# TensorE adds the experts' results and the residual in the last stage of a graph layer with experts

## The reference

```python
h = feats * rsqrt(deg_out)[:, None]
m = segment_sum(h[src], dst, n) * rsqrt(deg_in)[:, None]
x = (m @ W_gc + b_gc) + (feats @ W_res + b_res)
core = moe_ff(x, ...)        # each node's two best of 64 experts, weighted by their gates
y = x + core
mean = y.mean(axis=0); var = ((y - mean) ** 2).mean(axis=0)
out = (y - mean) * rsqrt(var + 1e-5) * gamma + beta
z = feats + out
result = (z - z.mean(axis=-1)) / sqrt(z.var(axis=-1) + 1e-5)
```

## Time and profile before

| | |
|---|---|
| median of three runs | 3374.38 us (3372.07 to 3375.9) |
| the profiled execution | 3370.39 us, its span 3368.7 us, 1.7 us around it |
| mean granted clock of TensorE | 0.940 |
| busy, share of the span | PE 83%, DVE 59%, ACT 36%, POOL 63% |
| `norms` | from about 3186 us to the end: 182 us |

### The profile page before, as it was taken

The page is one execution under the profiler, slowest core; times in us unless marked ns, Lnnn a source line. Parts: engine busy times, 40 slices in busy tenths (PEclk is TensorE's granted clock), DMA queues, the critical chain, the costliest instruction groups (busy, mean ns, idle before and its releaser), DMA issues. The chain is left out here.

```text
span 3368.7 us, 60861 instructions
## 1 busy us (share of the span) xinstructions
PE 2787.4 (83%) x15086; PEld 2055.8 (61%) x15227; DVE 1991.0 (59%) x6954; ACT 1201.6 (36%) x2876; POOL 2136.8 (63%) x2168
## 2 busy tenths in 40 slices
PE   4756888888888898888988889859999999999750
PEld 4534555555555555555555555539889889988640
DVE  6994555545555555555555556555555555555698
ACT  5982222222222222222222222214444444444339
POOL 5886777777777777777777777735555555555300
PEclk8877999999999999999999999979999999999885
DMA  7457454554545545455454554534444544444377
GB/s 238 150 180 229 134 160 136 158 168 135 158 137 158 168 135 159 138 157 167 135 160 135 158 168 126 162 119 131 157 137 140 165 144 132 145 145 134 136 300 250
DMA packets 305867, 533.96 MB, mean 159 GB/s; under 512 B 47156, under 2 KB 216729, under 8 KB 304046
## 3 DMA queue, kind: packets, MB, share of 16 engines
q0 software_dynamic: 102576, 273.86, 27.7%
q1 hardware_dynamic: 202734, 256.32, 22.8%
q10 hardware_dynamic: 400, 1.84, 0.2%
HBM read 416.19 MB, written 119.91 MB: 159 GB/s over the span
## 5 line engine op out<-in xcount | busy, mean ns | idle before, releaser
L1298 POOL DMA_INDIRECT work<-h_table,src_cols x1543 | 1466.3, 950 | 484.5 <-issue 461.2
L1688 PE MATMUL ps<-work 128*128 128x257 f32 x3322 | 1067.0, 404 | 244.2 <-DMA work<-h_table,src_cols 208.4
L1688 PEld LDWEIGHTS ps<-work 128*128 128x128 f32 x3322 | 574.3, 192 | 614.1 <-issue 472.8
L1830 POOL DMA_INDIRECT picked<-ys,places x228 | 250.0, 1097 | 357.7 <-DVE ys L1900 339.0
L1559 PE MATMUL ps<-none_w,none 128*128 128x512 bf16 x1244 | 476.3, 383 | 0.0
L1955 PEld LDWEIGHTS ps<-xst,work 128*128 128x128 f32 x3648 | 443.5, 192 | 28.0 <-issue 15.9
L1955 PE MATMUL ps<-xst,work 128*128 128x128 f32 x3648 | 447.3, 276 | 10.7 <-issue 10.0
L1962 PE MATMUL ps<-work,hid 128*128 128x256 f32 x1824 | 436.2, 382 | 0.3
L1811 ACT ACTIVATE hid<-ps,b_cols 128x128 f32<-128x128 f32 x912 | 316.7, 367 | 160.7 <-PE ps L1955 114.6
L1962 PEld LDWEIGHTS ps<-work,hid 128*128 128x128 f32 x1824 | 328.9, 190 | 45.7 <-ACT hid L1811 10.1
L1365 DVE TENSOR_TENSOR logits<-ps,gate_bias 128x64 f32<-128x64 f32 x98 | 22.0, 224 | 541.2 <-ACT acc L1253 541.2
(11 more groups left out here) (293 smaller groups left out, 4060.9 us busy)
## 6 DMA issues: line engine op xcount, KB each, us to landing
work<-in_L_gnn_w_dram SPq DMA_DIRECT2D x128, 512.0 KB, 4.6
picked<-work SPq DMA_DIRECT2D x14, 1792.0 KB, 8.1
work<-h_table,src_cols POOLq DMA_INDIRECT x1543, 2.8
pk<-picked SPq DMA_DIRECT2D x13, 1792.0 KB, 9.9
acc<-m_base SPq DMA_DIRECT2D x14, 903.0 KB, 4.9
x_beta<-xr_x SPq DMA_DIRECT2D x98, 128.0 KB
pk<-x_beta SPq DMA_DIRECT2D x14, 896.0 KB, 7.2
xr_x<-in_x_dram SPq DMA_DIRECT2D x97, 128.0 KB, 2.5
```

The lines of the kernel that those rows point to most:

```text
L1298: pool.indirect_dma_start(out=got[:, c % RING, 0:D], out_offset=None, in_=h_table[:, :], in_offset=bass.IndirectOffsetOnAxis(ap=src_cols[: ...
L1688: mm = nc.tensor.matmul(ps_flat[:, bank(t, k, w[0])], hot[:, (2 * t + (k >= HALF)) % HOTS, k % HALF if k >= HALF else k, :], got[:, c % RI ...
L1830: pool.indirect_dma_start(out=picked[:, :], out_offset=bass.IndirectOffsetOnAxis(ap=places[:, u:u + 1], axis=0), in_=ys[:, u, :], in_offse ...
```

## The change

In `aggregate` the addition of beta to feats becomes a `scalar_tensor_tensor` with an accumulator, so that each row's sum lands in `xb_sum`, kept in SBUF.

In the first pass TensorE takes the experts' results in pairs of tiles: four matmuls with the identity `ident` as weights put the sum of both experts' rows of two tiles into one bank of PSUM (of seven that take turns; the variance moves to the eighth). VectorE adds a pair from PSUM to `acc3` in one instruction of 512 columns, 49 in all; the two additions of seven tiles go. TensorE issues the pairs of group g+1 ahead of the folding of group g's squares. The buffers of `pk` are given back when the pairs are made (`paired`).

In the second pass `times_scale` becomes seven instructions, each of which also gives the row's sum; the mean comes from this sum and `xb_sum`. TensorE puts z = (x + beta) + scaled y into PSUM with two identity matmuls a tile, in two sets of four banks that alternate from group to group, and waits for `normed` of the group two before. ScalarE and VectorE read z from PSUM. ScalarE takes four tiles' deviations, VectorE three by `bn_stats`, with four small instructions to join the halves of each. In VectorE's order `minus_mean(g)` comes ahead of `spreads(g - 1)`, and `deviations(g)` ahead of `shifts(g - 1)`. ScalarE's order stays.

The diff, cut to its core (new semaphores, tiles and changed argument lists are left out):

```diff
@@ -1358,7 +1359,8 @@
...
                 dve.wait_ge(beta_in, 16)
-            nc.vector.tensor_tensor(xt[:, t % 2, :], xt[:, t % 2, :], beta_b[:, :], ALU.add).then_inc(beta_added, 1)
+            nc.vector.scalar_tensor_tensor(xt[:, t % 2, :], xt[:, t % 2, :], 1.0, beta_b[:, :], ALU.mult, ALU.add,
+                                           accum_out=xb_sum[:, t:t + 1]).then_inc(beta_added, 1)
...
@@ -1980,12 +1982,13 @@
...
 B = 4
-ON_ACT = 5
+ON_ACT = 4
 LAST_ON_ACT = 4
...
 UPFRONT = CENTRED + 2
-assert NT % GT == 0 and NG > B
+ZB = (GT + 1) // 2
+assert NT % GT == 0 and NG > B and NT % 2 == 0 and 2 * D <= BANK and 2 * ZB <= 8
 pk = t2("pk", [P, B, GT, TOP_K * D], F32)
...
@@ -2031,11 +2037,20 @@
...
-def adds(g):
-    return len(FIRST_PARTS) + g + (len(LAST_PARTS) - 1) * (g == NG - 1)
+def pairs_to(t):
+    return (t + 1) // 2
...
     return acc3[:, g * GT + u, 0:D]
+
+def pair_sum(i, b=2):
+    return ps[:, i % 7, 0:b * D]
+
+def z(g, u):
+    return ps[:, g % 2 * ZB + u // 2, u % 2 * D:(u % 2 + 1) * D]
+
+def z_ready(g, u):
+    return ZB * g + u // 2 + 1
...
@@ -2053,7 +2068,7 @@
...
             if g >= B:
-                sp.wait_ge(second_added, adds(g - B))
+                sp.wait_ge(paired, pairs_to(GT * (g - B + 1)))
             sp.dma_start(pk[:, g % B, :, :], rows_of(rows, g)).then_inc(pk_in[g % B], 16)
...
@@ -2076,11 +2091,11 @@
...
         for q in range(B):
-            sp.wait_ge(second_added, adds(NG - B + q))
+            sp.wait_ge(paired, pairs_to(GT * (NG - B + q + 1)))
             load_x(q)
...
             if g + B < NG:
-                sp.wait_ge(z_set, g + 1)
+                sp.wait_ge(z_done, ZB * (g + 1))
                 load_x(g + B)
...
@@ -2093,68 +2108,64 @@
...
         nc.vector.tensor_copy(last_ones[:, :], valid[:, NT - 1:NT].broadcast_to([P, P])).then_inc(last_ones_set, 1)
+        nc.vector.tensor_scalar(xb_sum[:, :], xb_sum[:, :], -1.0 / D, None, ALU.mult).then_inc(row_sums_set, 1)
+
         def centre(g):
...
-        def add(g, a, b, n):
-            nc.vector.tensor_tensor(group(g, a, b), group(g, a, b), pk[:, g % B, a:b, 0:D], ALU.add).then_inc(first_added, 1)
-            dve.wait_ge(first_added, n)
-            nc.vector.tensor_tensor(group(g, a, b), group(g, a, b), pk[:, g % B, a:b, D:2 * D], ALU.add).then_inc(second_added, 1)
+        def add(i):
+            dve.wait_ge(paired, i + 1)
+            rows = acc3[:, 2 * i:2 * i + 2, 0:D]
+            nc.vector.tensor_tensor(rows, rows, pair_sum(i).rearrange("p (u d) -> p u d", d=D), ALU.add).then_inc(added, 1)
...
             centre(g)
-        done = 0
-        for g in range(NG):
-            if g >= CENTRED:
-                dve.wait_ge(centred, g - CENTRED + 1)
-            if g > 0:
-                dve.wait_ge(pk_in[g % B], 16 * (g // B + (g % B > 0)))
-            for n, (a, b) in enumerate(FIRST_PARTS if g == 0 else parts(g)):
-                if g == 0:
-                    dve.wait_ge(first_in[n], 16)
-                done += 1
-                add(g, a, b, done)
-            if g + UPFRONT < NG:
-                centre(g + UPFRONT)
+        for i in range(NT // 2):
+            g, last = 2 * i // GT, (2 * i + 1) // GT
+            if last >= CENTRED:
+                dve.wait_ge(centred, last - CENTRED + 1)
+            add(i)
+            if (2 * i + 1) % GT >= GT - 2 and last + UPFRONT < NG:
+                centre(last + UPFRONT)
         dve.wait_ge(sq_used, NG - 1 + len(LAST_PARTS))
-        nc.vector.tensor_scalar(scale[:, :], ps[:, 1, 0:D], 1.0 / N, BN_EPS, ALU.mult, ALU.add).then_inc(var_set, 1)
+        nc.vector.tensor_scalar(scale[:, :], ps[:, 7, 0:D], 1.0 / N, BN_EPS, ALU.mult, ALU.add).then_inc(var_set, 1)
         dve.wait_ge(var_rooted, 1)
...
         dve.wait_ge(scale_set, 1)
-        dve.wait_ge(second_added, adds(NG - 1))
+        dve.wait_ge(added, NT // 2)
+        dve.wait_ge(row_sums_set, 1)
         def times_scale(g):
-            nc.vector.tensor_tensor(group(g), group(g), scale[:, :].unsqueeze(1).broadcast_to([P, GT, D]),
-                                    ALU.mult).then_inc(scaled, 1)
-
-        def residual(g):
-            dve.wait_ge(scaled, g + 1)
-            dve.wait_ge(xb_in[held(g)], 16 * (g // B + 1))
             for u in range(GT):
-                last = nc.vector.scalar_tensor_tensor(tile(g, u), tile(g, u), 1.0, pk[:, held(g), u, D:2 * D], ALU.mult, ALU.add,
-                                                      accum_out=z_sum[:, g % 2, u:u + 1])
-            last.then_inc(z_set, 1)
+                nc.vector.scalar_tensor_tensor(tile(g, u), tile(g, u), 1.0, scale[:, :], ALU.mult, ALU.mult,
+                                               accum_out=z_sum[:, g % 2, u:u + 1]).then_inc(scaled, 1)
         def minus_mean(g):
-            dve.wait_ge(z_set, g + 1)
-            nc.vector.tensor_scalar(z_mean[:, g % 2, :], z_sum[:, g % 2, :], -1.0 / D, None, ALU.mult).then_inc(z_mean_set, 1)
+            dve.wait_ge(scaled, GT * (g + 1))
+            nc.vector.scalar_tensor_tensor(z_mean[:, g % 2, :], z_sum[:, g % 2, :], -1.0 / D, xb_sum[:, g * GT:(g + 1) * GT],
+                                           ALU.mult, ALU.add).then_inc(z_mean_set, 1)
         def deviations(g):
-            dve.wait_ge(z_mean_set, g + 1)
-            if g >= B:
-                dve.wait_ge(o_out[held(g)], 16 * (g // B))
             for u in range(ON_ACT, GT):
-                last = nc.vector.scalar_tensor_tensor(pk[:, held(g), u, 0:D], tile(g, u), z_mean[:, g % 2, u:u + 1], tile(g, u), ALU.add, ALU.mult,
-                                                      accum_out=dev[:, g % 2, u:u + 1])
-            last.then_inc(dev_by_dve, 1)
+                dve.wait_ge(z_done, z_ready(g, u))
+                last = nc.vector.bn_stats(stats[:, u - ON_ACT, :], z(g, u))
+            last.then_inc(stats_set, 1)
+            dve.wait_ge(stats_set, 4 * g + 1)
+            own = dev[:, g % 2, ON_ACT:GT]
+            nc.vector.tensor_tensor(halves_gap[:, 0, :], stats[:, :, 1], stats[:, :, 4], ALU.subtract).then_inc(stats_set, 1)
+            nc.vector.tensor_tensor(own, stats[:, :, 2], stats[:, :, 5], ALU.add)
+            dve.wait_ge(stats_set, 4 * g + 2)
+            nc.vector.scalar_tensor_tensor(halves_gap[:, 1, :], halves_gap[:, 0, :], D / 4.0, halves_gap[:, 0, :], ALU.mult, ALU.mult).then_inc(stats_set, 1)
+            dve.wait_ge(stats_set, 4 * g + 3)
+            nc.vector.tensor_tensor(own, own, halves_gap[:, 1, :], ALU.add).then_inc(stats_set, 1)
         def spreads(g):
-            dve.wait_ge(dev_by_dve, g + 1)
+            dve.wait_ge(stats_set, 4 * (g + 1))
             dve.wait_ge(dev_by_act, g + 1)
...
@@ -2166,19 +2177,18 @@
...
             times_scale(g)
+            minus_mean(g)
             if g > 0:
                 spreads(g - 1)
-            residual(g)
-            minus_mean(g)
+            deviations(g)
             if g > 0:
                 shifts(g - 1)
-            deviations(g)
         spreads(NG - 1)
...
         for u in range(LAST_ON_ACT, GT):
-            nc.vector.tensor_scalar(pk[:, held(g), u, 0:D], tile(g, u), rstd[:, g % 2, u:u + 1], shift[:, g % 2, u:u + 1],
+            nc.vector.tensor_scalar(pk[:, held(g), u, 0:D], z(g, u), rstd[:, g % 2, u:u + 1], shift[:, g % 2, u:u + 1],
                                     ALU.mult, ALU.add).then_inc(normed_by_dve, 1)
...
@@ -2187,7 +2197,7 @@
...
             for n, (a, b) in enumerate(parts(g)):
-                act.wait_ge(second_added, len(FIRST_PARTS) + g + n)
+                act.wait_ge(added, pairs_to(g * GT + b))
                 nc.scalar.activation(sq[:, g % 2, a:b, :], group(g, a, b), ACT.Square).then_inc(squared, 1)
...
@@ -2197,7 +2207,8 @@
...
             for u in range(ON_ACT):
-                last = nc.scalar.activation(pk[:, held(g), u, 0:D], tile(g, u), ACT.Square, bias=z_mean[:, g % 2, u:u + 1],
+                act.wait_ge(z_done, z_ready(g, u))
+                last = nc.scalar.activation(pk[:, held(g), u, 0:D], z(g, u), ACT.Square, bias=z_mean[:, g % 2, u:u + 1],
                                             accum_out=dev[:, g % 2, u:u + 1])
...
@@ -2210,7 +2221,7 @@
...
             for u in range(LAST_ON_ACT if g == NG - 1 else GT):
-                nc.scalar.activation(pk[:, held(g), u, 0:D], tile(g, u), ACT.Identity, bias=shift[:, g % 2, u:u + 1],
+                nc.scalar.activation(pk[:, held(g), u, 0:D], z(g, u), ACT.Identity, bias=shift[:, g % 2, u:u + 1],
                                      scale=rstd[:, g % 2, u:u + 1]).then_inc(normed, 1)
...
@@ -2222,15 +2233,49 @@
...
     def _(pe):
+        def pair(i):
+            for n, (a, b) in enumerate(FIRST_PARTS):
+                if a == 2 * i:
+                    pe.wait_ge(first_in[n], 16)
+            g = (2 * i + 1) // GT
+            if g > 0 and (2 * i + 1) % GT < 2:
+                pe.wait_ge(pk_in[g % B], 16 * (g // B + (g % B > 0)))
+            if i >= 7:
+                pe.wait_ge(added, i - 6)
```

(47 more changed lines are left out.)

## The result

The changed kernel takes 3510.28 us (median of four runs, 3508.88 to 3512.04) beside 3374.18 us for the kernel before (four runs): ratio 1.0404, interval 1.0391 to 1.0416, so 136.1 us slower. The forecast was 3525.5, range 3500 to 3555. The profiled execution took 3512.04 us, 141.7 more than that of before.

What follows compares the result with a forecast made beforehand. TensorE was to bound the first pass, turns between z's halves the second: +62 first pass, +74.3 second, -3 PSUM normalisation, +18 clock, in all +151 on 3374.4, so 3525.5 us; range 3500 to 3555.

Steps and rivals of the forecast that it cites:

- The bound: First pass: TensorE's three products a tile bind from end to end, VectorE and loads fitting inside; +62.0 us.
- the turns: Second pass: the two halves of z alternate and never overlap, a period of 11.9 us a group; +74.3 us.
- the ring: Second pass: z(g-1) on TensorE, VectorE's last statistics and shifts, ScalarE's normalisations of g-2, then z(g); 11.9 us a turn.
- Rival (b): Second pass: halves of z overlap and TensorE binds, +8 us, with the first pass +62: 3444 us; chance 0.03.
- Rival (c): Second pass: clock stays at its lower level throughout, 92 us more in place of 18: 3600 us; chance 0.04.
- Rival (a): Both passes: identity matmuls at half price, one record of 0.235 us each: 3434 us; chance 0.03.
- Rival (d): Both passes: faster, VectorE was the bound and TensorE's work hides, -14 and -7 us: 3353 us; chance 0.02.
- The price of a product: Both passes: each f32 identity matmul, 128x128 by 128x256, costs TensorE 0.470 us at full clock.
- the term of 62.0: First pass: 138.2 us of TensorE products plus 2.7 for a cold start, ending at 3331.3 against 3269.3.
- +18: Second pass, clock term: three bursts of four lose 1.7 us to the lower clock; ends 0 and 38 us.
- The rest of the second pass: From the scale on: what 165.9 us holds beside TensorE's products, less 3 for ScalarE normalising out of PSUM.
- the step to the median: Whole kernel: the median of the runs was taken as 4.0 us above the profiled run.

Runs made afterwards that it cites:

- e3: Kernel before with only the changed first pass (pairs and their adds): 3418.4 us against 3374.0, ratio 1.0132.
- e5: Changed kernel without the second expert's rows in the first pass, results wrong: first pass 91.3 us against 129.35; whole run disturbed, 3961.8 us.
- e2: Changed kernel with VectorE issuing shifts(g-1) before deviations(g): 3440.9 us, second pass 117.1 us against 186.5.
- e7: Changed kernel with TensorE waiting for normalisations one bank (two tiles) at a time: second pass 143.8 us against 186.5; whole run disturbed, 3952.7 us.
- e1: Changed kernel with VectorE's and ScalarE's order in the second pass redone so the halves of z overlap: 3415.7 us, second pass 90.7 us.
- e10: Changed kernel with five extra products in each TensorE gap, wait for all seven kept: second pass 166.3 us against 186.5; whole run disturbed, 3986.3 us.
- e6: Kernel before with only the beta addition in the aggregation giving row sums, which nobody reads: 3369.3 us against 3369.4, ratio 0.9998.
- e11: Kernel before with TensorE summing two of seven tiles (groups 1 to 8), then adding x + beta for six of seven, orders recut: 3355.69 us against 3369.36.

## Why the prediction was right, point by point

**The bound and the turns held.** TensorE binds the first pass from end to end (e3, e5, and the window above). In the second the halves of z take turns, by the ring that was told: e2, e7 and e1 each break it at another place and get 69, 40 to 43 and 96 us back. Rival (b), a pass bound by TensorE alone, is what e1 made: 90.7 us, not what the changed order does. Rival (c), the lower clock throughout, did not occur (0.76). Rival (a) is refuted by the record counts and by e5. Rival (d) needed a product under 0.17 us. One reading of the prediction is wrong and changes nothing: VectorE does not square for the variance, ScalarE does (L2191 in the earlier trace rows), and but for the last group the row normalisation is ScalarE's as well. The groups came 13.2 to 13.66 us apart, at the upper end of the 12 to 13.5 named.

**The price of a product was mis-sized.** I divided 3.29 us by seven matmuls and got 0.470. The start-to-start distance is 0.432: the recorded end of a burst carries a tail of some 0.27 us, once. The trace of before had it, in a longer burst of the same line:

```profile
3262.95 5.88 PE L2231 MATMUL ps<-sq,ones 128*128 128x256 f32 x26 [0.70 <-ACT sq L2191]
```

Against the earlier trace rows, twelve records more take 5.88 - 3.29 = 2.59 us: 0.216 a record, 0.432 a matmul. With it the 294 products of the first pass come to 127.0 us; the first ten records, at the lower clock, take 4.39 us (3186.55 to 3190.94) for 2.16, which makes 129.2 of the 129.35 measured, and the term of 62.0 becomes 50.5. In the second pass the same error made 92.1 us of products out of 84.7.

**The clock was mis-sized the other way.** +18 was taken, three bursts of four at 1.7 us. Measured are 30: every burst from the third on starts low and loses 2.5 us (13.6 - 4.8 = 8.8 us long, for 8.05 - 1.76 = 6.3 in e2); the upper end was 38. The errors, -7.4 and +12 in the second pass and -11.5 in the first, partly cancel, and the experts' stage gives 4 us that no term had. That, and not each term, is why the forecast for the profiled execution, 3521.7, lies only 9.7 us above its 3512.0: the mechanism was right, but that the number came so close is in part luck. The other 5.5 of the 15.2 between the medians come from the step to the median, which was taken as 4.0 above the profile; it is 1.8 below it here.

The Trainium skill (Perfetto Trace Analysis, Matmul Optimizations) asks for matmuls back to back in batches, and by that rule the upper end was called the likelier. e2 and e10 agree with the rule: with a shorter or a filled gap the clock came to 0.99 and 0.92.

**The rest of the second pass**, its gaps and its ends, was reckoned at 70.8 (165.9 - 92.1 - 3) and came to 71.8 (186.5 - 84.7 - 30). Three `bn_stats` take 1.30 us in the turn above, 0.43 each, where 0.42 was taken. The seven normalisations out of PSUM take 3.16 us for the 3.44 of the earlier trace rows, 0.28 less where 0.23 (7 x 33 ns) was taken.

**In the aggregation** 0 was taken for the row sums, and e6 says 0.

## What to carry to other kernels

An f32 identity product costs 0.432 us for 128x256 here, and the sum of two operands takes two of them, 0.86 us a tile; VectorE adds the same tile in 0.28 to 0.29, or in 0.35 with a row sum or out of PSUM. So in the first pass TensorE spent 0.86 us a tile to spare VectorE some 0.2. An idle TensorE pays only for a share that leaves no engine far behind the others: with a share e11 is 0.4% faster than before, with the whole job e1 is 1.3% slower, its turns undone. Taking over the whole job moved the bound to TensorE: in the first pass that made it higher (129.35 us for 78.9), and in the second, with the turns undone, it gave 0.9 us (e1). Where two halves of a buffer are meant to overlap, follow each engine's queue around the ring once: one small step queued behind the wrong wait made the halves take turns and cost 69 us, more than the products of the first pass. When a pass gets shorter, look at what gives its buffers free: at 5.1 to 5.8 us a group the stores of four groups before began to hold ScalarE. Take a unit price from the difference between two bursts of different length, never from one burst divided by its count.

## What the runs showed of the hardware that I had not expected

Five more products in each gap made the pass shorter: 512 records took 166.3 us where 392 had taken 186.5, as the granted clock rose from 0.76 to 0.92 (2.4 GHz is 1.00). The twelve bursts of 28 records behind 4.8 us of idle all began at 1.2 GHz; behind 2.53 us those of e7 still did from the fourth burst on, and behind 1.76 us (e2) they began at full clock. The gap alone does not decide: behind gaps of 2.57 six of the twelve longer bursts of e10 lost time to the lower clock and six did not. An addition of two tensors by VectorE with one from PSUM costs no more than with both from SBUF (688 ns for 128x512 with PSUM, 684 to 693 without). VectorE's normalisation of the last group (`tensor_scalar`) does cost more: three tiles take 1.45 us out of PSUM (541 ns each, L2191) and 1.06 out of SBUF (411 ns, L2181 of before). ScalarE's normalisation is faster out of PSUM (573 ns against 586, seven in 3.16 us against 3.44).
